# Gate tiles fetched by one indirect DMA of 128 rows on GpSimd per step, in place of two broadcasts issued by SyncE

## The reference, cut to what matters

```python
def _L3_ffn_ref(x, gate_w, gate_b, w1, w2, w3):
    logits = einsum('bsd,de->bse', x, gate_w) + gate_b
    probs = softmax(logits)
    top_probs, top_idx = top_k(probs, 2)
    top_probs = top_probs / sum(top_probs)
    dispatch = sum(one_hot(top_idx, n_experts) * top_probs[..., None], axis=-2)
    h1 = einsum('bsd,edh->bseh', x, w1)
    h2 = einsum('bsd,edh->bseh', x, w2)
    hidden = silu(h1) * h2
    expert_out = einsum('bseh,eho->bseo', hidden, w3)
    return einsum('bseo,bse->bso', expert_out, dispatch)
# x here: the layer-normed tokens; the result is added to the residual that was normed
```

## Time and profile before

| | us |
|---|---|
| three runs | 2164.88, 2165.04, 2161.63 (median 2164.88) |
| the profiled execution | 2157.64 |
| its span, from the first to the last instruction | 2155.8 |
| PE busy | 1915.3 (89%) |
| DVE busy | 1104.9 (51%) |
| ACT busy | 951.8 (44%) |
| POOL busy | 697.7 (32%) |
| granted TensorE clock, mean | 0.926 |

### The profile page before, as it was taken

One profiled execution on the slowest core, in us unless ns is written; L12 is line 12 of the kernel. 1 busy time (PEld: TensorE's weight loads), 2 busy tenths in 40 slices (PEclk: granted clock), 3 DMA queues, 4 the chain that ended last, 5 costly groups with the idle time before them and its releaser, 6 DMA issues. The chain is left out here.

```text
span 2155.8 us, 31175 instructions
## 1 busy us (share of the span) xinstructions
PE 1915.3 (89%) x11979; PEld 1057.0 (49%) x11979; DVE 1104.9 (51%) x1331; ACT 951.8 (44%) x1323; POOL 697.7 (32%) x636
## 2 busy tenths in 40 slices
PE   7687999999697999945799998799999966999998
PEld 4553444444344444422544445576676743444444
DVE  4546667665713222275422223465565536766666
ACT  3333343434113666530466653366666632344433
POOL 0143444443112333341333331311121032444444
PEclk9888999999797999965799998899999987999999
DMA  4002333334001222110122222000000001333333
GB/s 101 1 1 81 104 101 102 102 102 124 0 1 36 75 77 77 64 25 0 26 76 78 76 65 66 1 2 1 1 2 1 2 3 47 107 107 107 113 105 93
DMA packets 71452, 121.28 MB, mean 56 GB/s; under 512 B 16954, under 2 KB 18554, under 8 KB 70658
## 3 DMA queue, kind: packets, MB, share of 16 engines
q1 hardware_dynamic: 71298, 119.20, 18.5%
HBM read 115.48 MB, written 3.67 MB: 55 GB/s over the span
## 5 line engine op out<-in xcount | busy, mean ns | idle before, releaser
L479 POOL TENSOR_TENSOR x<-x,mx_gated 128x512 f32<-128x512 f32 x256 | 326.2, 1274 | 402.5 <-DVE mx_gated L460 402.2
L443 ACT ACTIVATE mx_hidden<-mx_first 128x1024 f32<-128x1024 f32 x256 | 262.5, 1025 | 382.7 <-PE mx_first L357 382.7
L453 DVE TENSOR_TENSOR mx_hidden<-mx_second,mx_hidden 128x1024 f32<-128x1024 f32 x256 | 313.5, 1225 | 214.8 <-ACT mx_hidden L443 214.8
L558 ACT ACTIVATE mx_hidden<-mx_first,w_bias 128x1024 f32<-128x1024 f32 x256 | 271.1, 1110 | 168.5 <-PE mx_first L357 168.4
L571 DVE SCALAR_TENSOR_TENSOR mx_gated<-mx_out,w_bias,mx_gates 128x512 f32<-128x512 f32 x128 | 96.1, 751 | 361.6 <-PE mx_out L529 361.6
L419 PE MATMUL mx_out<-mx_hidden,w_second 128*64 128x512 f32 x1024 | 276.3, 618 | 1.3 <-DVE mx_hidden L453 1.3
L588 POOL TENSOR_TENSOR x<-x,mx_gated 128x512 f32<-128x512 f32 x128 | 164.2, 1283 | 323.1 <-DVE mx_gated L571 323.1
L529 PE MATMUL mx_out<-mx_hidden,w_second 128*64 128x512 f32 x1024 | 247.5, 605 | 0.0
L1468 DVE TENSOR_TENSOR c_near_weights<-c_near_hats 128x768 f32<-128x768 f32 x192 | 177.8, 967 | 133.2 <-PE c_near_turned L1348 133.2
L357 PE MATMUL mx_first<-tokens_high,first_high 64*128 64x512 f32 x1024 | 245.3, 475 | 0.9 <-ACT mx_hidden L558 0.6
L357 PEld LDWEIGHTS mx_first<-tokens_high,first_high 64*128 64x128 f32 x1024 | 96.8, 186 | 300.1 <-ACT mx_hidden L443 194.7
(11 more groups left out here) (219 smaller groups left out, 2434.4 us busy)
## 6 DMA issues: line engine op xcount, KB each, us to landing
mx_gates<-gate_board SPq DMA_DIRECT2D x768, 128.0 KB, 2.9
w_first<-in_f_first SPq DMA_DIRECT2D x4, 1024.0 KB, 11.8
c_weight<-in_c_weight SPq DMA_DIRECT2D x1, 2304.0 KB
x<-in_x SPq DMA_DIRECT2D x8, 256.0 KB, 4.3
w_second<-in_f_second SPq DMA_DIRECT2D x4, 512.0 KB, 13.3
w_first<-in_f_first SPq DMA_DIRECT2D x4, 512.0 KB, 9.8
out_x<-x SPq DMA_DIRECT2D x16, 128.0 KB, 2.4
gate_board<-xn SPq DMA_DIRECT2D x16, 64.0 KB, 2.6
```

The costliest lines, as they stand in the source:

```text
L443: act.activation(hidden[:, n % HIDDEN], first[:], ACT.Silu).then_inc(s.act.semaphore, 1)
L453: dve.tensor_tensor(own, second[:, n % SECOND], own, ALU.mult).then_inc(s.hidden.semaphore, 1)
L479: pool.tensor_tensor(place, place, gated[:, n % GATED, :], ALU.add).then_inc(s.added.semaphore, 1)
L558: act.activation(hidden[:, n % HIDDEN, f], first[:, f], ACT.Gelu, bias=w.bias1[:, e * F + f:e * F + f + 1]).then_inc(s.act.semaphore, 1)
```

## The change

POOL now fetches the gate tile with an indirect DMA: a list of 128 row numbers, one for each partition (`places`, column e: row e for the upper half, row E + e for the lower), says which row of the board goes to each partition. One DMA fills all 128 partitions. The source of the indirect DMA is a whole DRAM tensor, so each chunk has a board of its own (`boards[i]`). The call moves from SP's program to POOL's: four fetches ahead of the first add, and then one fetch ahead of each add, for the step that lies three steps later. SP keeps `post` and the stores. The two lists are constants loaded with `identity` and `countdown` in the first layer norm.

```diff
+AHEAD = 3
@@ class Gates
-        self.board = k.board[0:HALVES * E, :]
+        self.boards = [board[0:HALVES * E, :] for board in k.boards]
+        self.places = k.places[E]
     def post(self, sp, i):
         self.s.rows.wait(sp, i + 1)
-        sp.dma_start(self.board[:, chunk(i)], self.rows[:, chunk(i)]).then_inc(self.s.posted.semaphore, 16)
-
-    def spread_out(self, sp, n):
+        if i >= 1:
+            self.s.gated.wait(sp, (i - 1) * self.E + 1)
+        sp.dma_start(self.boards[i], self.rows[:, chunk(i)]).then_inc(self.s.posted.semaphore, 16)
+
+    def spread_out(self, pool, n):
         i, e = n // self.E, n % self.E
         if e == 0:
-            self.s.posted.wait(sp, 16 * (i + 1))
+            self.s.posted.wait(pool, 16 * (i + 1))
         if n >= self.SLOTS:
-            self.s.gated.wait(sp, n - self.SLOTS + 1)
-        for h in range(HALVES):
-            row = h * self.E + e
-            sp.dma_start(self.spread[half(h), n % self.SLOTS, :],
-                         self.board[row, chunk(i)].partition_broadcast(C)).then_inc(
-                             self.s.gate[n % self.SLOTS].semaphore, 16)
+            self.s.gated.wait(pool, n - self.SLOTS + 1)
+        pool.indirect_dma_start(self.spread[:, n % self.SLOTS, :], None, self.boards[i],
+                                bass.IndirectOffsetOnAxis(ap=self.places[:, e:e + 1], axis=0)).then_inc(
+                                    self.s.gate[n % self.SLOTS].semaphore, 16)
     def wait(self, dve, n):
-        self.s.gate[n % self.SLOTS].wait(dve, 16 * HALVES * (n // self.SLOTS + 1))
+        self.s.gate[n % self.SLOTS].wait(dve, 16 * (n // self.SLOTS + 1))
     def serve(self, sp, last_layer):
         for n in range(CHUNKS * E):
             i, e = n // E, n % E
-            self.spread_out(sp, n)
             if e == E // 2 and i + 1 < CHUNKS:
                 self.post(sp, i + 1)
@@ mixture_swiglu and mixture_gelu, both
     @block.gpsimd
     def _(pool):
+        for n in range(AHEAD):
+            gates.spread_out(pool, n)
         for n in range(STEPS):
+            if n + AHEAD < STEPS:
+                gates.spread_out(pool, n + AHEAD)
             s.gated.wait(pool, n + 1)
             if n >= 1:
                 s.added.wait(pool, n)
@@ lay_out
+        c[f"places{E}"] = (np.repeat(np.arange(HALVES), C)[:, None] * E + np.arange(E)[None]).astype(np.uint32)
```

More of the change, by code:

```diff
@@ L144, in _ @@
             if turn == 0:
-                pe.wait_ge(k.more_constants, 16 * 2)
+                pe.wait_ge(k.more_constants, 16 * 4)
         @block.scalar
@@ L345, in count @@
         for gate in s.gate:
-            gate.base += 16 * HALVES * (steps // self.SLOTS)
+            gate.base += 16 * (steps // self.SLOTS)
         for signal, count in ((s.turned, CHUNKS), (s.rows, CHUNKS), (s.posted, 16 * CHUNKS), (s.gated, steps),
@@ L2017, in build @@
         k.gate = sb("gate", [P, HALVES * TILES * SWIGLU.experts])
-        k.board = nc.dram_tensor("gate_board", (HALVES * SWIGLU.experts, N), F32, kind="Internal").ap()
+        k.boards = [nc.dram_tensor(f"gate_board{i}", (HALVES * SWIGLU.experts, CHUNK), F32, kind="Internal").ap()
+                    for i in range(CHUNKS)]
         k.centring = sb("centring", [P, P])
@@ L2037, in build @@
         k.w.bias2 = sb("w_bias2", [P, GELU.experts])
+        k.places = {m.experts: sb(f"places{m.experts}", [P, m.experts], mybir.dt.uint32)
+                    for m in (SWIGLU, GELU)}
         k.w.loaded = ctx.enter_context(nc.semaphore("w_loaded"))
@@ L2052, in build @@
                    (k.countdown[:], ins["countdown"], k.more_constants)]
+        k.loads += [(k.places[m.experts][:], ins[f"places{m.experts}"], k.more_constants) for m in (SWIGLU, GELU)]
         turn = 0
@@ L2087, in lay_out @@
     }
+    for m in (SWIGLU, GELU):
+        E = m.experts
+        c[f"places{E}"] = (np.repeat(np.arange(HALVES), C)[:, None] * E + np.arange(E)[None]).astype(np.uint32)
     p = "L0_conv_"
```

## The result

| | before | after |
|---|---|---|
| median of 5 runs each, us | 2161.63 | 2171.18 |
| lowest to highest | 2158.8 to 2165.04 | 2169.85 to 2172.51 |
| the profiled execution, and its span | 2157.64, 2155.8 | 2172.51, 2170.6 |
| granted TensorE clock, mean | 0.926 | 0.924 |

The ratio after to before is 1.0049, 95% interval 1.0032 to 1.0066: slower by 7 to 14 us. The forecast was 2229. Its direction holds, its size and its reason do not.

A forecast was written before the change was run, and what follows sets the result against it. PE was taken to bound the mixtures; POOL's fetches at 1.63 us would add 32.1 and 32.5 in the SwiGLU mixtures, +64.6 on 2157.64, so 2222, plus 7.2 to the median: 2229 us. Range 2159 to 2480.

The forecast's parts named there:

- What bounds the kernel: In the mixtures PE sets the pace; removing SP's 768 broadcasts, 456 us of issue time, was given no gain.
- D = 1.63: Time one fetch holds POOL in a mixture step: two SP issues, 1.19 us, plus 0.446 for reading the list.
- +64.6: Total us added to the profiled execution's 2157.64, all from the first and fourth mixtures.
- The bounds, 0.59 and 2.9: Limits for D in us: one issue on SP from below, an issue through to landing from above.
- The threshold of 1.38, and no gap between an add and a fetch: SwiGLU mixtures slow only if D exceeds 2.65 - 1.27 = 1.38 us, POOL running adds and fetches without idle between.
- "no change" rival: D under 1.38 us, so POOL hides the fetch in its 1.33 us of idle; time 2165, chance 0.37.
- +32.1 and +32.5 in the SwiGLU mixtures: First and fourth mixtures grow to 371.7 us each, from 339.6 and 339.2, at 2.904 us per POOL step.
- GELU mixtures 0: Second and third mixtures unchanged: POOL needs 2.91 us a step against 3.54 available.
- start of a mixture 0: Four fetches before the first add move it from 182.58 to 183.9 us, adding nothing to the total.
- landing not limiting: At the first mixture's start the first gate tile lands at 181.3 us, before DVE wants it at 181.82.
- The prediction's own sign for it: Adds in the SwiGLU mixtures still 2.60 us apart would show the forecast wrong, with D below 1.38.
- The others: Rivals: D 2.3 to 2.9, 2406 to 2636 us, chance 0.16; list read singly, 6300, 0.02; faster, 2158 at best, 0.05.

The follow-up runs named there:

- The two doubled experiments: Changed kernel with two 64-row fetches in place of each 128-row one, 2429.38 us; changed kernel with a second, unread 128-row fetch behind each, 2447.64 us.
- the best, without the drains: Changed kernel without POOL's drain at the ends of the mixtures and of the small block `start_at_one`: 2159.07 against 2157.95 us for the kernel before, ratio 1.0000.
- the broadcasts: Changed kernel with two direct 64-row broadcasts per step, issued by POOL, in place of each indirect fetch: 2181.12 us.

## Why the prediction was wrong in size, step by step

- **What bounds the kernel**: right. PE's busy time in the mixtures is unchanged, and taking 456 us of issues from SP gave nothing (ratio 1.0000 once no drain is waited for).
- **D = 1.63**: this failed, and with it all of the forecast's +64.6. It was put as twice an issue of SP plus 0.446 for the list; it is 0.969. On POOL the rows cost 0.001 us each and the rest, with the list, is a fixed 0.85. If an issue on SP is made up alike, which no run shows, twice an issue charged its fixed part twice. The bounds, 0.59 and 2.9, held. The Trainium skill's figure was the better guide: the prediction's estimate of about 1.0 from "DMA: Bandwidth & Descriptors", section Specifications, is near the measured 0.969, though the page gives about 1 us as the time to the first byte and not as the time for which the engine is held. The Trainium skill's "Perfetto Trace Analysis", section DMA Instruction — SWDGE (GPSIMD), has the profile's bar of such a DMA end when its descriptors are written and not when its data have landed; the trace agrees (0.97 against 3.8 to the landing, median), so 2.9 as an upper end was a reading of the wrong thing.
- **The threshold of 1.38, and no gap between an add and a fetch**: the shape is right, the size off. A fetch starts 0.16 behind an add, and the next add 0.02 behind the fetch, so the room for D in a step of 2.60 us is 2.60 - 1.29 - 0.16 - 0.02 = 1.13. The margin that is left is 0.16 us a step (2.60 against 2.44), far less than the "no change" rival assumed. The earlier trace rows showed two compute instructions in a row, which says nothing of a DMA.
- **+32.1 and +32.5 in the SwiGLU mixtures**: measured +0.32 and -0.16, since D is below the threshold. The term is simply not there. The two doubled experiments show that it would have been, had POOL needed more than a step's time.
- **GELU mixtures 0, start of a mixture 0, landing not limiting**: right within 0.1 us, and the first add comes at 183.00 where 183.9 was worked out with the larger D.
- **A step that was never priced**: the end of a block. The prediction asked "who is queued behind POOL's fetch", and stopped at the last add. POOL's drain was in the program in every block; before, with no DMA of POOL behind it, it ended 0.1 us after the last add, and the adds' rows do not show it. It is all of the loss: +1.50, +5.24, +5.24. The fourth mixture's drain takes 1.50 us more too (2.846 us from 2166.00), but it ends at 2168.8, before the output's last store lands at 2170.2, and so 3.3 us lie behind the last add as before.
- **The rivals**: "no change", D under 1.38, had the right mechanism for the mixtures and the wrong time; its 2165 leaves out 12 us of drains. The prediction's own sign for it came, adds still 2.60 us apart. The others did not occur. So slower came true for a reason that no case had, and that it did was luck.
- **Slips in the sum**: the two ends of the forecast's case were worked out unlike. At D = 2.3 the sum under the rivals gives 2406, and the paragraph on the numbers has 2413, with the 7.2 in twice. That 7.2, from the profiled execution to the median, came from three runs; with five it is 4.0, and in the later groups of 15 to 23 runs the kernel before has medians of 2157.46 to 2158.24, level with the profiled execution. In the sentence on small reads, 10.9 us a fetch make some 3.5 ms more and not 3.7.

What stays open: what exactly the drain does for each DMA, and why its price starts anew at 110 or so fetches of 128 rows and at 122 DMAs of 64 rows. The counts, the drains' durations and the pauses are shown. That one store explains them is a reading, not a thing seen, and it has to say why the two doubled kernels got the lower price without a pause.

No version here beats the kernel before: the best, without the drains, is level with it at 1.0000.

## What to carry to other kernels

When a DMA moves to GpSimd, price three things: how long it holds the engine (here 0.97 us and 0.15 to 0.30 beside it), whether that fits in the engine's idle time in each step, and what the next drain behind it costs (0.082 us for each DMA since the last clearing) if a barrier waits for it. The last does not show as work of any engine and not in a timeline. Look for stretches at the stage boundaries in which nothing runs, compare them before and after, and ask the trace for the drains by the line of the block's end. A removed cost that nobody waited for pays for nothing, however many microseconds of issue it was.

## What the runs showed of the hardware that was not expected

- POOL's drain costs 0.082 us for each DMA that POOL issued since the last clearing, for indirect and direct ones alike, whether the last was issued 163 us or 2.3 us before the last add's end; at 64 it is 5.24 us (the drain instruction takes 6.60 in place of 1.36).
- The price does not grow without end: 128 fetches of 128 rows cost 1.50, 256 DMAs of 64 rows 1.01. In the kernel after and with the broadcasts, POOL's stream has a pause of 0.85 us before the 114th fetch, or of 2 us before the 129th and the 251st broadcast. In the two doubled kernels it has none. The 0.7 us by which the first is longer than usual is far less than the 8.85 us that a drain costs after 108 fetches.
- An indirect DMA of 128 rows of 2 KB holds POOL for 0.969 us, one of 64 rows 0.907, a direct one of 64 rows 0.526 where SP takes 0.594 in the median.
